# Last layer norm of a two-layer graph network: twelve blocks normed on ScalarE inside the loop, reciprocal roots as exponentials of logarithms, last transposes ahead of the projections

## What is computed

```python
x = _layernorm(x + _L0_gnn_ref(x, adj, pairs, Wq, bq, Wk, bk))     # sparse attention over listed pairs
x = _layernorm(x + _L1_gnn_ref(x, adj, W_seq, a1, a2, W_out, b_out))

def _layernorm(x, axis=-1, eps=1e-05):
    m = jnp.mean(x, axis=axis, keepdims=True)
    v = jnp.var(x, axis=axis, keepdims=True)
    return (x - m) / jnp.sqrt(v + eps)

def _L1_gnn_ref(...):
    seq = (x @ W_seq).reshape(N, H, DH)                 # 16 heads of 32
    scores = leaky_relu(score1[:, :, None] + score2[:, None, :])
    attn = softmax(scores + (1.0 - adj)[None] * MASK_VAL, axis=-1)
    hidden = einsum('hij,jhd->ihd', attn, seq).reshape(N, D_IN)
    return jax.nn.elu(hidden @ W_out + b_out)
```

## Time and profile before

| | |
|---|---|
| median of 3 runs | 505.12 us (503.98 to 505.14) |
| the profiled execution's own time | 506.74 us |
| its span, first to last instruction | 505.0 us |
| mean granted clock of TensorE | 0.883 of full |
| busy: PE, DVE, ACT, POOL | 377.3, 334.2, 193.1, 185.3 us |
| instructions | 5236 |

### The profile page before, as it was taken

How to read it: one execution, slowest core, us unless ns; L and a number is a source line. 1 busy time by engine, 2 the same in 40 slices (tenths; PEclk the granted TensorE clock), 3 DMA queues, 4 the chain that set the end, 5 groups by cost and what they waited for, 6 DMA issues and landing times.

```text
span 505.0 us, 5236 instructions
## 1 busy us (share of the span) xinstructions
PE 377.3 (75%) x1646; PEld 199.7 (40%) x1646; DVE 334.2 (66%) x879; ACT 193.1 (38%) x414; POOL 185.3 (37%) x208
## 2 busy tenths in 40 slices
PE   1761021216999999699799988937899999999961
PEld 1320000003545544345378866812444444444430
DVE  2983000004398756489677778576899999999683
ACT  4830000005646472132245543421124646465732
POOL 7777777720000001000000000047887778784000
PEclk9995555557999999899999999967899999999986
DMA  7994000002243459732191111146666565553062
GB/s 279 380 324 151 0 0 0 0 0 83 81 136 119 167 132 254 137 64 84 45 351 45 66 43 66 63 117 186 172 180 182 155 168 161 163 156 107 0 251 89
DMA packets 37062, 65.11 MB, mean 129 GB/s; under 512 B 17952, under 2 KB 19104, under 8 KB 34976
## 3 DMA queue, kind: packets, MB, share of 16 engines
q1 hardware_dynamic: 27936, 42.46, 25.8%
q0 software_dynamic: 9088, 22.20, 16.3%
HBM read 53.50 MB, written 8.52 MB: 123 GB/s over the span
## 4 chain that ended last, share of the span: by engine, by line
PE 38%; issue 26%; POOL 22%; DVE 8%; DMA 2%; ACT 2%; POOLq 0%; SPq 0%; DVEq 0%; ACTq 0%
POOL avals L492 15%; PE ps L890 11%; PE ps L817 11%; PE ps L784 10%; POOL adjT L576 5%; DMA arenaA<-in_x_dram,curi 2%; PE ps L647 1%; PE ps L773 1%; PE ps L609 1%; PE ps L808 1%; POOL stage L564 1%; PE ps L764 1%; DVE arenaC L1644 1%; DVE stats L1650 1%; DVE arenaA L1215 1%
## 5 line engine op out<-in xcount | busy, mean ns | idle before, releaser
L609 PE MATMUL ps<-arenaB,adjT 128*128 128x512 f16 x512 | 126.4, 401 | 49.6 <-issue 35.1
L576 POOL DMA_INDIRECT adjT<-seqtab,eidx x80 | 82.5, 1032 | 153.9 <-DMA seqtab<-scores 132.0
L609 PEld LDWEIGHTS ps<-arenaB,adjT 128*128 128x128 f16 x512 | 51.1, 102 | 118.8 <-issue 50.0
L890 PE MATMUL ps<-adjT,stage 128*128 128x512 f32 x160 | 80.1, 642 | 11.9 <-DVE adjT L1823 11.9
L492 POOL DMA_INDIRECT avals<-in_adj_dram,aidx x79 | 76.5, 968 | 23.9 <-issue 23.9
L1211 DVE TENSOR_TENSOR arenaA<-iota,halves 128x2048 f16<-128x2048 f16 x15 | 18.3, 1223 | 80.7 <-ACT halves L938 71.2
L947 ACT COPY adjT<-ps 128x1024 f16<-128x1024 f16 x22 | 21.3, 1014 | 110.2 <-remote 83.9
L784 PE MATMUL ps<-stage 128*128 128x272 f32 x256 | 61.5, 394 | 1.5 <-ACT stage L1033 1.5
L817 PE MATMUL ps<-adjT 128*128 128x512 f32 x128 | 59.5, 609 | 4.0 <-ACT adjT L1054 4.0
L1823 DVE TENSOR_TENSOR adjT<-adjT 128x512 f32<-128x512 f32 x80 | 53.8, 734 | 1.8 <-ACT adjT L1132 1.2
L784 PEld LDWEIGHTS ps<-stage 128*128 128x128 f32 x256 | 47.4, 190 | 10.8 <-ACT stage L1033 2.0
(11 more groups left out here) (256 smaller groups left out, 491.2 us busy)
## 6 DMA issues: line engine op xcount, KB each, us to landing
stage<-in_adj_dram SPq DMA_DIRECT2D x16, 1024.0 KB
arenaA<-in_x_dram SPq DMA_DIRECT2D x4, 1024.0 KB
seqtab<-arenaA SPq DMA_DIRECT2D x16, 256.0 KB, 2.0
out_dram<-arenaC SPq DMA_DIRECT2D x16, 256.0 KB, 2.6
arenaB<-in_x_dram SPq DMA_DIRECT2D x1, 1536.0 KB, 10.8
adjT<-seqtab,eidx POOLq DMA_INDIRECT x80, 3.8
avals<-in_adj_dram,aidx POOLq DMA_INDIRECT x79
arenaC<-in_L_gnn_Wq_dram SPq DMA_DIRECT2D x1, 1024.0 KB
```

Of the source, the lines that this page charges most:

```text
L576: g.indirect_dma_start(out=G[:, b % GR, k, :], out_offset=None, in_=seqtab, in_offset=bass.IndirectOffsetOnAxis(ap=eidx[:, b * KE + k:b * ...
L609: ins = t.matmul(bank(4 + b % 2), adjT[:, b, j, :], xsplit[:, w, j, :], start=(j == 0 and w == 0), stop=(j == NB - 1 and w == 1))
L890: t.matmul(bank(2 + b % 2), ehot[:, b % 2, k, :], G[:, b % GR, k, 0:D], start=False, stop=(k == KE - 1), skip_group_check=True)
```

## The change

- ScalarE preloads one table set with both the exponential and the logarithm ahead of the second layer. The reciprocal root is now exp(-0.5 ln(v + eps)), two activations (`last_roots`), in place of a square root on ScalarE and a reciprocal on VectorE. The unused root goes.
- `spread_of` has a fourth step: it makes a second share of the sum, so that the sum of squares comes out as the variance.
- ScalarE norms blocks 0 to 11 itself (`norm_of`): a shift of 128 x 1 and one activation with scale and bias. In the loop stand the roots of two blocks in every even turn from 6 and a norm in every turn from 7 (blocks 0 to 8); the norms of 9 to 11 stand between the last steps. They count `fin_a`; SyncE waits for it ahead of the first twelve stores.
- VectorE norms only blocks 12 to 15, each behind the next block's add_elu.
- TensorE transposes block 14 ahead of the projection of block 13, and block 15 ahead of that of block 14. ScalarE's last steps stand in a new order, the copy of block 14 first.

```diff
@@ sizes
+    LAST = NB - 4
@@ SyncE
             for b in range(NB):
-                sp.wait_ge(fin, b + 1)
+                if b < LAST:
+                    sp.wait_ge(fin_a, b + 1)
+                else:
+                    sp.wait_ge(fin, b - LAST + 1)
                 sp.dma_start(out[b * P:(b + 1) * P, :], x1[:, b, :]).then_inc(stored, 16)
@@ TensorE, behind the loop
-                    project(NB - 3)
-                    for b in range(NB - 2, NB):
-                        pe.wait_ge(e_hid, b + 1)
-                        turn_hidden(b)
-                        project(b)
+                    pe.wait_ge(e_hid, NB - 1)
+                    turn_hidden(NB - 2)
+                    project(NB - 3)
+                    pe.wait_ge(e_hid, NB)
+                    turn_hidden(NB - 1)
+                    project(NB - 2)
+                    project(NB - 1)
@@ ScalarE, spread_of
                 s.activation(mv[:, b, 0:1], stats[:, b, 0:1], ACT.Identity, scale=-1.0 / D).then_inc(stat, 1)
-                act.wait_ge(stat, 3 * b + 2)
-                s.activation(zt[:, b % 2, :], x1[:, b, :], ACT.Square, bias=mv[:, b, 0:1],
+                s.activation(stats[:, b, 1:2], stats[:, b, 0:1], ACT.Identity, scale=-float(D) ** -1.5).then_inc(stat, 1)
+                act.wait_ge(stat, 4 * b + 3)
+                s.activation(zt[:, b % 2, :], x1[:, b, :], ACT.Square, bias=stats[:, b, 1:2], scale=float(D) ** -0.5,
                              accum_out=mv[:, b, 1:2]).then_inc(stat, 1)
@@ ScalarE, new or changed helpers
-            def last_roots(lo, hi, measured):
-                act.wait_ge(var_made, measured)
-                s.activation(rstd[:, 0, lo:hi], mv[:, lo:hi, 1], ACT.Sqrt, bias=bias[:, 1:2]).then_inc(last_root, 1)
+            def last_roots(lo, hi, k):
+                s.activation(rstd[:, 0, lo:hi], mv[:, lo:hi, 1], ACT.Ln, bias=bias[:, 1:2]).then_inc(log_made, 1)
+                act.wait_ge(log_made, k + 1)
+                s.activation(rstd[:, 1, lo:hi], rstd[:, 0, lo:hi], ACT.Exp, scale=-0.5).then_inc(last_root, 1)
+            def norm_of(b):
+                act.wait_ge(last_root, b // 2 + 1)
+                s.activation(stats[:, b, 2:3], mv[:, b, 0:1], ACT.Identity, scale=rstd[:, 1, b:b + 1]).then_inc(shift_made, 1)
+                act.wait_ge(shift_made, b + 1)
+                s.activation(x1[:, b, :], x1[:, b, :], ACT.Identity, bias=stats[:, b, 2:3],
+                             scale=rstd[:, 1, b:b + 1]).then_inc(fin_a, 1)
@@ ScalarE, second layer
                 with act.If(misfit < 1):
+                    s.preload_act_table_set("natural_log_exp_and_others")
...
                         if b >= 2:
                             lay_bias(b - 2)
-                    spread_of(NB - 5)
-                    act.wait_ge(stat, 3 * (NB - 4))
-                    s.activation(rstd[:, 0, 0:NB - 4], mv[:, 0:NB - 4, 1], ACT.Sqrt, bias=bias[:, 1:2],
-                                 scale=1.0 / D).then_inc(last_root, 1)
-                    for b in range(NB - 4, NB - 2):
-                        elu_part(b, NB - 4)
+                        if b >= 6 and b % 2 == 0:
+                            act.wait_ge(stat, 4 * (b - 4))
+                            last_roots(b - 6, b - 4, b // 2 - 3)
+                        if b >= 7:
+                            norm_of(b - 7)
+                    copy_turned(NB - 2)
+                    spread_of(LAST - 1)
+                    elu_part(NB - 4, LAST)
+                    lay_bias(NB - 2)
+                    last_roots(LAST - 2, LAST, LAST // 2 - 1)
+                    elu_part(NB - 3, LAST)
+                    copy_turned(NB - 1)
+                    lay_bias(NB - 1)
+                    norm_of(NB - 7)
+                    act.wait_ge(var_made, NB + 1)
+                    last_roots(LAST, LAST + 1, LAST // 2)
+                    norm_of(NB - 6)
+                    elu_part(NB - 2)
+                    act.wait_ge(var_made, NB + 2)
+                    last_roots(LAST + 1, LAST + 2, LAST // 2 + 1)
+                    norm_of(NB - 5)
+                    elu_part(NB - 1)
                     for b in range(NB - 2, NB):
-                        lay_bias(b)
-                        copy_turned(b)
-                        elu_part(b)
-                    s.activation(gate[:, 5:6], bias[:, 1:2], ACT.Sqrt)
-                    last_roots(NB - 4, NB, NB + 4)
+                        act.wait_ge(var_made, b + 5)
+                        last_roots(b, b + 1, LAST // 2 + b - LAST)
@@ VectorE, in place of last_scales and last_norms
+            def last_norm(b, roots):
+                dve.wait_ge(last_root, roots)
+                v.tensor_scalar(x1[:, b, :], x1[:, b, :], mv[:, b, 0:1], rstd[:, 1, b:b + 1], ALU.subtract,
+                                ALU.mult).then_inc(fin_a if b < LAST else fin, 1)
@@ VectorE, behind the loop
                 finish(NB - 1)
-                last_scales(0, 0, NB - 4)
-                last_norms(0, 2, ALU.add)
-                add_elu(NB - 4, late)
-                last_norms(2, 7, ALU.add)
-                add_elu(NB - 3, late)
-                last_norms(7, NB - 4, ALU.add)
-                add_elu(NB - 2, late)
-                add_elu(NB - 1, late)
-                last_scales(1, NB - 4, NB)
-                last_norms(NB - 4, NB)
+                add_elu(LAST, late)
+                for b in range(LAST + 1, NB):
+                    add_elu(b, late)
+                    last_norm(b - 1, LAST // 2 + b - LAST)
+                last_norm(NB - 1, LAST // 2 + NB - LAST)
```

More of the change, by code:

```diff
@@ L224, in two_layer_graph_attention @@
             sem(n) for n in ("o_load", "h_turned", "h_evac", "z_made", "z_neg", "z_exp", "z_used"))
-        last_root = sem("last_root")
+        last_root, log_made, shift_made, fin_a = (sem(n) for n in ("last_root", "log_made", "shift_made", "fin_a"))
         bias_laid = sem("bias_laid")
@@ L1070, in elu_part @@
                 if measured > 0:
-                    act.wait_ge(stat, 3 * measured)
+                    act.wait_ge(stat, 4 * measured)
                 s.activation(zt[:, b % 2, :], bank(6 + b % 2), ACT.Relu, scale=-1.0).then_inc(z_neg, 1)
@@ L1170, in act_second_layer @@
                         elu_part(b)
-                    last_roots(0, NB - 4, 2 * NB - 4)
-                    last_roots(NB - 4, NB, 2 * NB)
+                    act.wait_ge(var_made, 2 * NB)
+                    last_roots(0, NB, 0)
             count = how_many(act)
@@ L1725, in _ @@
             mB = M2[:].unsqueeze(1).to_broadcast([P, NB, H1])
-            def last_scales(k, lo, hi):
-                dve.wait_ge(last_root, k + 1)
-                link(v.reciprocal(rstd[:, 1, lo:hi], rstd[:, 0, lo:hi]))
-            def last_norms(lo, hi, shift=ALU.subtract):
-                for b in range(lo, hi):
-                    v.tensor_scalar(x1[:, b, :], x1[:, b, :], mv[:, b, 0:1], rstd[:, 1, b:b + 1], shift,
-                                    ALU.mult).then_inc(fin, 1)
+            def last_norm(b, roots):
+                dve.wait_ge(last_root, roots)
+                v.tensor_scalar(x1[:, b, :], x1[:, b, :], mv[:, b, 0:1], rstd[:, 1, b:b + 1], ALU.subtract,
+                                ALU.mult).then_inc(fin_a if b < LAST else fin, 1)
             def by_head(rows):
@@ L1922, in _ @@
                     add_elu(b, late)
-                last_scales(0, 0, NB - 4)
-                last_scales(1, NB - 4, NB)
-                last_norms(0, NB)
+                for b in range(NB):
+                    last_norm(b, 1)
             assert links[0] == one_end
```

2 lines of the change are left out of this document (1 added, 1 removed).

## The result

Medians of four runs each, taken together: 504.55 us before (503.01 to 505.14), **498.02 us** after (497.23 to 498.45). The ratio is 0.989 with a 95% interval of 0.9854 to 0.9926: 6.5 us faster, where 6.4 were forecast.

A forecast was written before the change was run, and what follows sets the result against it. TensorE paces the loop (8.60 us a turn) and waits behind ACT's copies in the tail. Terms +4.6, -0.7, -0.4, 0, +1.4, +1.5 make 6.4 us: 498.7 us against the median of 505.12; 8-in-10 range 497.4 to 501.5.

The forecast's parts named there:

- The loop costs nothing: Second layer's loop: ACT's added 1.4 us (odd turns) or 1.9 (even) is covered by DVE's lead over TensorE; cost 0.
- TensorE 4.6 earlier: Tail: project(15) gives its result at 489.7 instead of 494.30 on the old trace, 4.6 us earlier.
- ACT 0.7 late: Tail: ACT's norms, roots and elu run to 490.4, so the last elu starts 0.7 us late.
- Roots for nothing: Tail: logarithm and exponential (0.30 + 0.20) in place of root and reciprocal change the time by 0.
- table loads for nothing: Three table loads of 1.28 us each go, one stays ahead of the loop; worth nothing on the path.
- Norms +1.4: End of the tail: one norm behind the last root and not four, 1.4 us gained.
- DVE -0.4: Tail: DVE has last_norm(13) ahead of add_elu(15), 0.4 us lost.
- The store, +1.5: After the last norm: the end comes 3.0 us behind it, not 4.56; 1.5 gained, bounds +0.8 and +2.1.
- Rival 1: Tail: TensorE's clock at half level slows project(14), giving 499.9 us, or 501.7 with project(15) slow too; chance 0.25.
- Rival 3: Loop: ACT overruns it and the kernel is slower, about 515 us with table switches; chance 0.05.

The follow-up runs named there:

- three norms on DVE: The changed kernel with the norms of blocks 9 to 11 on VectorE in place of ScalarE: 417.37 us, ratio 0.9864 to the kernel before.
- new order alone: The kernel before with only the new order of the last turns, keeping square roots, reciprocals and VectorE's norms: 423.9 us, ratio 1.0015 to the kernel before.
- the two repeats: The changed kernel itself, unaltered, run two more times: 497.27 and 497.23 us, ratios 0.9867 and 0.9886 to the kernel before.
- table switches: The changed kernel without the table set preload, so a table load stands ahead of each logarithm and each exponential behind it: 515.3 us, ratio 1.0261 to the kernel before.
- norms and roots, old order: The changed kernel with the old order of the last turns on TensorE and of ScalarE's last copies and biases: 420.7 us, ratio 0.9949 to the kernel before.

## Why the prediction was right, and where it was lucky

Its steps, moved by -2.28 us (474.38 against 476.66, the start of what follows the sums), against the trace of after:

| step | forecast | measured |
|---|---|---|
| copy_turned(14) ends | 475.6 | 475.65 |
| spread_of(11) ends | 477.5 | 477.44 |
| lay_bias(14) ends | 480.1 | 480.16 |
| project(14) starts | 480.26 | 480.21 |
| lay_bias(15) ends | 483.1 | 483.11 |
| project(15)'s result | 487.4 | 487.34 |
| last relu starts | 488.1 | 488.14 |
| last norm ends | 493.2 | 493.03 |

- **The loop costs nothing: shown.** The chain ahead of the relu measured 1.99 us, for 2.0, but that match is luck: the prediction's own terms for an even turn, 0.49, 0.53 and 1.17, make 2.19, by which the weights would have been 0.1 us late and not 0.1 early. The norm's term of 1.17 measured 1.04 (0.814 for the large activation, reckoned as 0.82; the next one starts 0.09 ahead of its end), the pair of roots 0.44, lay_bias 0.52. The slack in one turn was not what made it safe anyway. One activation of 0.64 more in each turn breaks that slack and costs nothing either; the cover is the lead, 5.1 us at block 15. The 0.85 + 8 x 0.57 = 5.4 that follows from the prediction's figures is near it by two errors that cancel: three traces of the changed kernel start with 1.9 to 2.2 at block 7, and the lead grows by some 3 from there and not by 4.6. The stores in the loop are nine, blocks 0 to 8, not twelve.
- **TensorE 4.6 earlier, ACT 0.7 late: shown.** The first by the table (block 15's result is ready 17.44 us behind the sums before and 12.80 after); 1.7 of it is the stretch at the half level that the old trace had and the new one hasn't, which the prediction counted in by taking project(14) at full clock. The second measured 0.80, and three norms on DVE gave back 0.49 at the relu and 0.58 at the last norm.
- **Roots for nothing, table loads for nothing: true of this order only.** The prediction called the load at 474.72 worth nothing on the path, and that holds in the old order. With the new order alone lay_bias(14) comes 2.57 us later, the two loads of 1.28 for the most part, the half level costs another 1.70, and no gain is left. The prediction missed that the new order needs the loads gone.
- **Norms +1.4, DVE -0.4: near.** From the last relu to the end of the last norm it is 4.89 us, and 6.14 before: 1.25, where 1.0 was reckoned. The last norm is alone, with another one of 0.52 ahead of the last add_elu.
- **The store, +1.5: mis-sized, +1.2** (4.56 to 3.37; in the two repeats 3.6 and 3.4 behind the norm, where 3.0 was reckoned). It is inside its bounds of +0.8 and +2.1. The median landing of the earlier trace rows was too kind: from the last store's start to the end it is 3.35 us (493.05 to 496.4), and the old trace had 3.6 there.
- **The whole:** three comparisons gave 6.5, 6.0 and 5.3 us, each with an interval of about 2 to 3 us to either side, against 6.4. The tail is 6.1 to 6.3 shorter in three traces of the changed kernel, but all against one trace of the old one, with its 1.7 at the half level. That the first median met the forecast within 0.1 is in part luck, and in the tail +0.2 between relu and norm and -0.3 in the store nearly cancel.
- **Rival 1, the half clock: did not come.** A pause of 1.32 to 1.36 us was followed by the full level in the three traces of the changed kernel and in that with one more activation, one of 1.59 as well. By these five, 0.25 looks high, though no run excludes it.
- **Rival 3, the overrun:** its price was near (18.0 against 16.3 above the base), but its break-even was not. It let DVE lose 12.4 us before the kernel is no faster; 12.9 us of waits gave a kernel that is 6.1 us slower than before. The term that failed is a cost in the tail, put at nothing, that measured 4.5 us, 3.1 of them at the half level; the lead also absorbed 4.7 and not 6. In the price of the table switches the tail had its part, and that part was near (10.7 expected later, 10.8 measured).

## What to carry to other kernels

An engine's slack in one turn is not the limit for what can be added beside a loop: the limit is the lead that the engine it feeds has built up by the end, and once that is spent the tail pays too. Before crediting a reordering, list what stands between the moved steps on the busiest engine of the tail: here table loads and a measurement that could have gone into a 3.5 us gap decided between a gain of 0, 6 and 8 us. Test the parts apart, since two halves worth 3.3 and 0.4 in the tail were worth 6.3 together. And look at the granted clock in each trace that you compare: one stretch at the half level was worth 1.7 us here, about as much as the norms alone.

## What the runs showed of the hardware

- **The same program, 80 us apart.** On one chip the kernel before takes 423.03 us, on the others 502.5 to 505.12. The difference arises in the first layer, between some 30 and 115 us. Windows of TensorE, DVE, ACT and GpSimd on the slower kind of chip (changed kernel; columns as in the earlier trace rows):

```profile
40.00:110.00 70.00, 12.77 (x35) 3.41 (x33) 7.54 (x29) 0.00 (x0) 49.84 (x53) 0.52 0.15 46
```

and on the faster (norms and roots, old order):

```profile
40.00:110.00 70.00, 69.39 (x431) 36.77 (x429) 57.37 (x168) 41.19 (x51) 54.15 (x53) 1.00 0.48 153
```

In those 70 us TensorE, DVE and ACT hardly start anything on the one chip. A row of TensorE in after:

```profile
71.74 0.58 PE L613 MATMUL ps<-arenaB,adjT 128*128 128x512 f16 x1 [2.22 <-issue]
```

It starts one matmul every 2.80 us and waits for nothing that the profile names. GpSimd runs nearly alike on both (53 instructions, 49.84 and 54.15 us busy). What holds the issue is not known; it is worth twelve times the change, and this study didn't try to remove it.

- **The clock after a pause has no single answer.** After 1.32 to 1.59 us the level stayed full in five traces; after 2.00 us it was half once and full three times; after 1.91 half and after 1.92 full, in one trace (table switches); after 3.9, partly half in both cases.
- **A table load took 1.28 us and no more** in the trace of the table switches, and whether the compiler puts one between a logarithm and an exponential hangs on one preload: 18 us for this kernel.
